# Four places of a two-layer transformer kernel: GpSimd in the V projection, the FFN's way out, the head of the expert stage, and gates turned one FFN later

## The reference, cut to what matters

```python
x = layernorm(x + attention0(x))    # 16 heads of 64, softmax over 1024 keys, V = x @ Wv
x = layernorm(x + ffn0(x))          # own layernorm, dequantised weights, silu, 128-512-128
x = layernorm(x + attention1(x))    # one head of 128 over 512-token batches
n = rmsnorm(x) * norm_weight        # normalised tokens of the expert stage
probs = sigmoid(n @ router_w.T); top-2 of 8, weights normalised -> gates
x = layernorm(x + ffn_shared(n) + sum_e gate_e * ffn_e(n))   # nine FFNs 128-512-128, relu
```

## Time and profile before

| | us |
|---|---|
| median of 3 runs | 1094.57 |
| lowest and highest | 1093.62, 1097.33 |
| the profiled execution | 1092.86 |
| its span | 1091.1 |
| PE busy | 1031.3 (95%) |
| DVE busy | 836.5 (77%) |
| POOL busy | 719.2 (66%) |
| ACT busy | 638.2 (58%) |

### The profile page before, as it was taken

How to read it: one execution, slowest core, us unless ns; L and a number is a source line. 1 busy time by engine, 2 the same in 40 slices (tenths; PEclk the granted TensorE clock), 3 DMA queues, 4 the chain that set the end, 5 groups by cost and what they waited for, 6 DMA issues and landing times. The chain is left out here.

```text
span 1091.1 us, 25198 instructions
## 1 busy us (share of the span) xinstructions
PE 1031.3 (95%) x7983; PEld 858.1 (79%) x7983; DVE 836.5 (77%) x1493; ACT 638.2 (58%) x1311; POOL 719.2 (66%) x736
## 2 busy tenths in 40 slices
PE   5889999999999999999999999887998799999996
PEld 4678888888888888888888888655686677777774
DVE  5977878878877877877877887656765589898896
ACT  4655655555556556556556565564443577666774
POOL 4167877877877877877877878611323387777772
PEclk9999999999999999999999999899899799999998
DMA  6143443543543543543543543110000012112111
GB/s 127 42 100 86 100 101 85 104 96 85 106 94 86 110 92 84 113 89 83 116 86 82 119 93 69 45 31 2 0 1 19 1 61 97 58 66 69 59 40 38
DMA packets 57041, 80.09 MB, mean 73 GB/s; under 512 B 25956, under 2 KB 38048, under 8 KB 55968
## 3 DMA queue, kind: packets, MB, share of 16 engines
q1 hardware_dynamic: 54792, 78.97, 31.7%
q10 hardware_dynamic: 2208, 0.59, 0.3%
HBM read 19.43 MB, written 1.11 MB: 19 GB/s over the span
## 5 line engine op out<-in xcount | busy, mean ns | idle before, releaser
L670 POOL TENSOR_TENSOR probs_lo<-probs 128x512 f16<-128x512 f32 x384 | 392.3, 1040 | 159.2 <-ACT probs L470 157.7
L470 ACT ACTIVATE probs<-bank_s 128x512 f32<-128x512 f32 x512 | 309.4, 605 | 263.1 <-PE bank_s L389 259.5
L511 DVE TENSOR_REDUCE maxes<-bank_m 128x1 f32<-128x512 f32 x512 | 353.1, 690 | 137.8 <-PE bank_m L301 128.5
L382 PE MATMUL bank_s<-qa,ka 128*128 128x512 f32 x512 | 228.4, 446 | 5.1 <-DVE arena L559 2.5
L301 PE MATMUL bank_m<-ka,qa 128*128 128x512 f32 x512 | 208.2, 407 | 3.4 <-DMA ka<-tk_lo 2.6
L389 PE MATMUL bank_s<-qb,kb 65*128 65x512 f32 x512 | 207.1, 404 | 0.9 <-DMA qb<-negmax 0.9
L324 PE MATMUL bank_o<-v_now,probs 128*128 128x129 f16 x2048 | 201.7, 221 | 0.3 <-ACT o_parts L436 0.3
L1386 POOL TENSOR_TENSOR hidden_lo<-rectified,hidden_hi 128x512 fp32r<-128x512 f32 x112 | 156.5, 1415 | 66.7 <-ACT hidden_hi L1558 56.6
L324 PEld LDWEIGHTS bank_o<-v_now,probs 128*128 128x128 bf16 x2048 | 176.2, 98 | 21.5 <-issue 20.4
L320 PE MATMUL bank_o<-v_now,probs_lo 128*128 128x65 f16 x2048 | 185.8, 193 | 0.0
L301 PEld LDWEIGHTS bank_m<-ka,qa 128*128 128x128 f32 x512 | 158.6, 310 | 31.5 <-issue 4.4
(11 more groups left out here) (271 smaller groups left out, 1704.0 us busy)
## 6 DMA issues: line engine op xcount, KB each, us to landing
qa<-tq_hi SPq DMA_DIRECT2D x64, 256.0 KB, 4.2
v_now<-arena SPq DMA_DIRECT2D x32, 260.0 KB, 2.3
ka<-tk_hi SPq DMA_DIRECT2D x32, 256.0 KB, 3.0
ka<-tk_lo SPq DMA_DIRECT2D x32, 256.0 KB, 5.1
kb<-tk_hi SPq DMA_DIRECT2D x32, 256.0 KB, 5.1
qb<-tq_lo SPq DMA_DIRECT2D x32, 256.0 KB, 5.2
gates_on_all<-gate_rows SPq DMA_DIRECT2D x8, 1024.0 KB, 4.6
e_raw<-in_L_ffn_ew_dram SPq DMA_DIRECT2D x16, 256.0 KB, 3.1
```

The source lines that it names most:

```text
L382: nc.tensor.matmul(bank_s[u % 2][:], ka[h][:, ks], qa[h][:, qs], start=True, stop=False)
L470: nc.scalar.activation(probs[:, c, u, :], bank_s[u % 2][:], ACT.Exp, scale=SCALE).then_inc(exp_done, 1)
L511: nc.vector.tensor_reduce(maxes[:, j // 2, j % 2:j % 2 + 1], bank_m[j % 2][:], AX.X, ALU.max).then_inc(m_reduced, 1)
L670: nc.gpsimd.tensor_tensor(probs_lo[:, c, u, :], p, hi, ALU.subtract).then_inc(lo_pool, 1)
```

## The change

In the set-up, POOL makes `wv_lo`, and every fourth lo of V (units 3, 7, ... 31, eight of 32): ACT, after its hi, copies the bank to SBUF (`v_copy`), and POOL subtracts from there. In the FFN, DVE does both late `enter`s before the first `leave`, and both last `finish`es after the last `leave`. In the last step of attention nothing is turned or split any more, POOL no longer normalises X there, and DVE's second token chunk comes last. The expert stage turns and splits chunks 0 and 1 itself, with POOL making their lo. Routing comes after tile (2, 1) of FFN 0, turning the gates after chunk 0 of FFN 1; POOL normalises X in four places spread over FFNs 1, 2 and 7; DVE splits FFN 1's weights before it chooses gates. FFNs 1 and 2 stand unrolled ahead of the loop.

```diff
+        V_BY_POOL = [n for n in range(V_N) if n % 4 == 3]
+        v_copy = probs[:, 0, 4:6, :]
@@ PE, V units
-                    if n >= 4:
-                        pe.wait_ge(vlo_done, n - 3)
+                    if n - 4 in V_BY_POOL:
+                        pe.wait_ge(v_copied, by_pool_upto(n - 4))
+                    elif n >= 4:
+                        pe.wait_ge(vlo_done, n - 3 - by_pool_upto(n - 4))
@@ ACT, V units
+                    if n in V_BY_POOL:
+                        k = by_pool_upto(n) - 1
+                        if k >= 2:
+                            act.wait_ge(vlo_pool, k - 1)
+                        nc.scalar.copy(v_copy[:, k % 2, :], bank_v[n % 4][:]).then_inc(v_copied, 1)
+                act.wait_ge(vlo_pool, len(V_BY_POOL))
@@ POOL, set-up
+                pool.wait_ge(wvhi_ready, 1)
+                nc.gpsimd.tensor_tensor(wv_lo, wv_raw, wv_hi.bitcast(F32), ALU.subtract).then_inc(wvlo_ready, 1)
...
+                for k, n in enumerate(V_BY_POOL):
+                    pool.wait_ge(v_copied, k + 1)
+                    pool.wait_ge(vhi_done, n + 1)
+                    nc.gpsimd.tensor_tensor(V[...lo of unit n...], v_copy[:, k % 2]..., V[...hi...], ALU.subtract).then_inc(vlo_pool, 1)
@@ quantised_ffn, DVE
-            leave(0)
-            finish(0)
-            enter(2)
-            enter(3)
-            for c in range(1, CHUNKS):
+            for c in range(LATE, CHUNKS):
+                enter(c)
+            for c in range(LATE):
                 leave(c)
+                finish(c)
+            for c in range(LATE, CHUNKS):
+                leave(c)
+            for c in range(LATE, CHUNKS):
                 finish(c)
@@ attend_once, DVE
-                    if step == STEPS and kt in (1, 3):
-                        normalise_tokens(nc, dve, X, persist["n_tok"], ln, kt // 2)
-            dve.wait_ge(ln["nt_hi_ready"], 1)
-            nc.vector.tensor_tensor(nt_lo[:, 0:CH], ...)
+                    if step == STEPS and kt in (3, 7):
+                        normalise_tokens(nc, dve, X, persist["n_tok"], ln, kt // 4)
@@ mix_experts
-        ROUTE_AT, GATES_AT = 1, 3
+        ROUTE_AT, GATES_AT = (2, 1), (1, 0)
+        HI_AT = {(1, 1): 2, (2, 0): 3}
+        INPUT_AT = {(1, 0): 0, (1, 3): 1, (2, 2): 2, (NE - 1, 1): 3}
@@ mix_experts, POOL
-            nc.gpsimd.memset(y_sum[:], 0.0).then_inc(lane_ready, 1)
+            nc.gpsimd.memset(gates[0][:], 1.0).then_inc(gates_in[0], 16)
+            for c in range(LATE):
+                pool.wait_ge(hi_ready, c + 1)
+                nc.gpsimd.tensor_tensor(nt_lo[:, cs], nt[:, cs], nt_hi[:, cs].bitcast(F32), ALU.subtract).then_inc(lo_ready, 1)
@@ mix_experts, PE
-            times_wo(LATE)
-            turn_tokens(1)
-            for c in range(LATE + 1, CK):
-                times_wo(c)
+            for c in range(LATE):
+                times_wo(LATE + c)
+                turn_tokens(c)
@@ mix_experts, DVE
-            add_and_sum(nc, dve, X, ln, LATE, bank_y[LATE])
-            take_lo(1)
-            add_and_sum(nc, dve, X, ln, LATE + 1, bank_y[LATE + 1])
             for c in range(LATE, CK):
+                add_and_sum(nc, dve, X, ln, c, bank_y[c])
                 normalise_tokens(nc, dve, X, n_tok, ln, c)
-            nc.vector.memset(gates[0][:], 1.0).then_inc(gates_in[0], 16)
...
+                    split_weights(1, 1)
                     choose_gates()
-                    split_weights(1, 1)
```

More of the change, by code:

```diff
@@ L828, in out_root @@
                 act.wait_ge(out_moments, c + 1)
-                nc.scalar.activation(out_std[:], out_mv[:, :, 1], ACT.Sqrt, bias=eps[:, 2:3]).then_inc(out_rooted, 1)
+                nc.scalar.activation(out_std[:, c, :], out_mv[:, c, :, 1], ACT.Sqrt, bias=eps[:, 2:3]).then_inc(out_rooted, 1)
             for c in range(2):
@@ L1151, in _ @@
                         times_wo(WO_AT[step, kt])
-                    if step == STEPS and kt == TB - 3:
-                        turn_tokens(0)
         @block.scalar
@@ L1184, in _ @@
                                              scale=rden[:, g % 4:g % 4 + 1]).then_inc(o_scaled, 1)
-                    if step == STEPS and kt == TB - 3:
-                        act.wait_ge(ln["n_turned"], 1)
-                        nc.scalar.activation(nt[:, 0:CH], bank_a[0][:], ACT.Copy, scale=nw).then_inc(ln["nt_ready"], 1)
-                        act.wait_ge(ln["nt_ready"], 1)
-                        nc.scalar.copy(nt_hi[:, 0:CH], nt[:, 0:CH]).then_inc(ln["nt_hi_ready"], 1)
                 if step == STEPS - 1:
@@ L1386, in ffn @@
                         nc.gpsimd.tensor_tensor(h_lo[:, f, :], r[:, f, :], h_hi[:, f, :].bitcast(F32), ALU.subtract).then_inc(lo_pool, 1)
-                if first_ffn:
-                    for c in range(LATE, CK):
-                        normalise_input(nc, pool, X, ln, c)
+                    if first_ffn and c == 0:
+                        nc.gpsimd.memset(y_sum[:], 0.0).then_inc(lane_ready, 1)
+                    if isinstance(n, int) and (n, c) in INPUT_AT:
+                        normalise_input(nc, pool, X, ln, INPUT_AT[n, c])
             over_ffns(pool, ffn)
@@ L1533, in _ @@
             biases(0, 0)
-            act.wait_ge(turned, 2)
-            nc.scalar.activation(nt[:, CH:2 * CH], bank_y[1][:], ACT.Copy, scale=nw).then_inc(nt_ready, 1)
-            take_hi(1)
-            root_of_variance(nc, act, ln, LATE, 1e-8)
+            for c in range(LATE):
+                act.wait_ge(turned, c + 1)
+                nc.scalar.activation(nt[:, c * CH:(c + 1) * CH], bank_y[c][:], ACT.Copy, scale=nw).then_inc(nt_ready, 1)
+                take_hi(c)
+                if c == 0:
+                    root_of_variance(nc, act, ln, LATE, 1e-8)
             def rectify(n, half, c, f):
@@ L1569, in ffn @@
                                 root_of_variance(nc, act, ln, LATE + 1, 1e-8)
-                            if c < 2 and f == 3:
-                                take_hi(c + 2)
+                            if (c, f) in HI_AT:
+                                take_hi(HI_AT[c, f])
+                            if (c, f) == ROUTE_AT:
+                                act.wait_ge(routed, 1)
+                                nc.scalar.activation(prob[:].rearrange("p t e -> p (t e)"), bank_c[1][:, 0:T * NE],
+                                                     ACT.Sigmoid).then_inc(gated, 1)
                         elif f - 1 in (0, 2):
@@ L1575, in ffn @@
                             split_weights(n + 1, 1 - half)
[L1576 to L1579 removed]
+                    if isinstance(n, int) and (n, c) == GATES_AT:
                         for g in range(CK):
```

62 lines of the change are left out of this document (28 added, 34 removed).

## The result

| | before | changed |
|---|---|---|
| median of 5 runs | 1094.57 | 1089.51 |
| lowest and highest | 1093.62, 1097.33 | 1088.92, 1090.00 |
| span of the profiled execution | 1091.1 | 1088.2 |

A forecast was written before the change was run, and what follows sets the result against it. PE was taken as the bound, busy 95% of the span, with time to win only where it idles or runs at half clock. 3.0 + 0.6 + 1.8 + 10.8 = 16.2 gave 1078 on the scale of medians, range 1071 to 1085.

The forecast's parts named there:

- A: Set-up: `wv_lo` and some lo's of V on POOL start V earlier and speed it up; 3.0 saved.
- B: Way out of the FFN: DVE's new order of enters and finishes shortens the tail behind PE's end; 0.6 saved.
- C1: End of attention: no `nt_lo`, turning or copies there, and the second token chunk last; 1.8 saved.
- C2: Head of the expert stage: FFN 0's stall goes and gates are chosen earlier, so FFN 2 begins earlier; 10.8 saved.
- S': The start of the expert stage in the changed kernel, from which the forecast counted its times there.
- the fourth bullet of C2: From DVE's start in FFN 1 to FFN 2: 20.7 before, forecast 18.6; FFN 2 at S' + 57.6 against 68.9.
- the paragraph on the gates: Gates land at S' + 47.2, needed at S' + 49.4; turning them behind chunk 0 of FFN 1 costs PE nothing.
- the gates' own slack of 2.2: FFN 1: time between the gates' landing, S' + 47.2, and DVE's need of them at chunk 2, S' + 49.4.
- POOL blocks DVE for longer: Rival: normalising X beside weight splits in FFNs 1 and 2 takes 4 to 5 off C2, about 1082; chance 0.07.
- the 2.1 that was to come back: Between DVE's start in FFN 1 and FFN 2: uncovered part of POOL's 6.0 on X, expected to be regained.
- The clock at half around routing: Rival: half clock from routing to FFN 0's end leaves C2 at 7, total 12, about 1083; chance 0.20.
- The slower one: Rival: a late choice stalls PE in FFN 1, or late gates stall DVE at chunk 2; 1099 if 26 late; chance 0.03.

The follow-up runs named there:

- e4: The changed kernel, but SP asks for the weights of FFN 2 ahead of storing and loading the gates; median 1084.10, ratio 0.9913 to the kernel before.
- e8: The changed kernel with no lo of V on POOL (`wv_lo` stays there); median 1089.31, ratio 0.9960 to the kernel before.
- e1: The kernel before with the set-up part of the change alone; median 1091.83, ratio 0.9983 (0.9961 to 1.0004).
- e7: The changed kernel with the gates turned behind chunk 3 of FFN 0, as before the change; median 1086.88, ratio 0.9941 to the kernel before.
- e5: e4 with POOL normalising only 4 of 128 columns of X, to price that work; median 1076.52, ratio 0.9839 to the kernel before.
- e6: e4 with X normalised in eight single steps instead of four double ones, none beside DVE's weight split; median 1084.27, ratio 0.9914 to the kernel before.
- e9: e4 with X normalised early on POOL: end of attention, start of expert stage, FFNs 0 and 1; median 1079.65, ratio 0.9871 to the kernel before.
- e11: The changed kernel measured again unaltered, as a control; median 1087.71, ratio 0.9950 to the kernel before, span 1081.6.

## Why the prediction was wrong

**What held.** A: V's start (15.8 forecast, 15.4), the wait for the first head (1.6, 1.66), the last product at 42.4 at the full clock (42.1 forecast; e4) and 43.8 with the fall behind that wait, DVE's 1.79 without POOL's share (e8). Forecast 3.0, by `e1` 2.3 in the median (not clear of noise) and 3.2 to 3.5 in the trace at the second head. The trace of the result, with 2.25 there, is the exception: in the nine others with this set-up the clock kept its level behind the wait for the first head, and the second head's maximum comes at 52.1 to 53.0. The second head's DMA takes a part that I left out (a wait of 4.27 instead of 1.91). B: 0.6, measured 0.7. C1: 1.8, and 1.6 by the ledger (2.85 against 1.25). C2 up to DVE's start in FFN 1: S' + 39 forecast, 37.3 measured. That is the expected gain, and it was there: 13.6 in all when FFN 1 begins.

**The step that failed** is the fourth bullet of C2 and the paragraph on the gates, "From there to FFN 2 it was 911.42 - 890.73 = 20.7 ... 18.6". It was 25.9 (902.86 - 876.97), by the first two of the three things below; the third cost more in the FFNs behind it, for which I had taken 0.5 off.

- *The turn itself had no price.* I asked whether PE waits for the choice ("it costs nothing while these 5 to 6 last"), and it doesn't. But the 20.7 were taken from a kernel in which the turn lay ahead of FFN 1; moved behind chunk 0 it lies inside the 18.6. It takes 2.8; where it was it took 2.3 before, and 2.2 in `e7`.
- *A queue that the gates were moved past.* SP has one list, and the weights stand behind the gates in it. In the kernel before they were asked for at once behind the load of the earlier trace rows, 3.7 behind FFN 1's first product (886.82), and ACT came to split them 14.5 behind it. With the gates' later turn they are asked for 12.2 behind it, and ACT comes 15.6 behind (892.29 - 3.48) and waits; I costed the gates' own slack of 2.2 and never asked what stands behind them. It costs 3.6 in chunk 2 of FFN 1, by `e4` 4.2 in the whole of it.
- *X on POOL.* I took 0.5; by `e5` against `e4` it is 6.1 in the traces, 1.5 of it by a fall of the clock. The rival "POOL blocks DVE for longer" had the mechanism, at least in part, and nearly the size (4 to 5), and 0.07: in `e6` PE's four waits of 0.3 and more inside FFNs 2 and 3 end with DVE's subtraction, in the changed kernel with DVE's split and with POOL's lo's. Both arguments against it were wrong. "POOL is busy for 66% of the span on the page, so its additions fit" asks for room on the wrong engine: single steps do fit between POOL's lo's (`e6`, 20.12 busy of 23.00), but DVE beside them is busy for 23.00 of 23.00. A pair at once also makes the lo's behind it late. And "most DVE work in an FFN reads PSUM" is not so: of the five operations of a chunk only the gating does, 16.3 of the 120.9 for which DVE was busy from 892 to 1020 before, in this row:

```profile
L1652 DVE SCALAR_TENSOR_TENSOR y_gated<-bank_y,e_bias_now,gates_on_all 128x512 f32<-128x512 f32 x22 | 16.3, 740 | 0.0
```

The others, two hi's, the sum and the lo, work in SBUF, as X does on POOL. Before, two of the four chunks were done at the end of attention, where `e9` shows them to be free; I had counted POOL's work there as saving nothing, which is right, and its new place as costing next to nothing, which isn't (but for the pair behind the turn).

By the ledger, in spans: A 2.2 (forecast 3.0); the first layer's FFN -1.0 (0.6; its own 0.7, less 1.7 for one fall of the clock); C1 1.6 (1.8); from the start of the expert stage to FFN 2 5.7 (11.3; 1.7 better up to DVE's start, less 2.8 for the turn, about 4.2 for the weights, and a rest of 0.3: of the 2.1 that was to come back with X leaving its old place, the second chunk of FFN 1 shows 1.6); from there to the end -5.7 (-0.5). That is 2.9, the difference of the two spans. The medians differ by 5.1, since the execution profiled before was 1.7 below its median and that of the changed kernel 0.5 above its own.

**The rivals.** The clock at half around routing occurred in some traces and not in others (the same 32 matmuls in 4.37 and 3.63, in two traces of one kernel), and costs 2.7. It came in the trace of the result, but FFN 1 began with the expected lead all the same, so it isn't the cause of the miss; and the one profiled run without it took 1083.4 (e11), still 5 above the forecast. The slower one, PE waiting for the choice or DVE for the gates, did not happen. With both losses mended as far as `e9` does, the time is 14.3 below that of before in its session, within the range that was forecast. That doesn't confirm the sum: the turn (2.8) and X in FFN 1 (2.8) still cost there, and the way to FFN 1 was better than its term. That version beats both kernels; 2.8 of X in FFN 1 is left in it.

What stays open: why the granted clock falls twice, once or never in the same stage of the same kernel. I can say what a fall costs, not what brings it. It isn't chance alone: the mean granted clock was 0.976 over the 74 runs of the kernel before, 0.979 over the 11 of the changed one, and 0.982 to 0.983 with weights first (e4, e5), so part of each gain came by fewer falls. Also open is how the cost of a pair of steps divides between POOL's late lo's and the DVE that it holds; for single steps in FFNs 2 and 3 PE's waits name DVE alone.
